# A windowed-attention and binary-FFN layer on one core: the order of the first and last attention blocks

## The chip, the cores and the metric

One core of a Trainium2 chip. The metric is the device time of one launch in microseconds (us); before the change the median of three runs was 380.07 us (380.04 to 381.41).

## The reference

A post-norm transformer layer over x of 4096 tokens x 256, all in float32:

```
q, k = l2norm(x Wq'), l2norm(x Wk')        16 heads of 16
v = x Wv'
p = softmax(q k' + bias)     bias = -slope[h]*|i-j|, -1e30 where j < i or j - i >= 128 (i query, j key)
x1 = layernorm(x + (p v) Wo')
bw = mean|w| over a row * sign(w)          for w1 (1024 x 256) and w2 (256 x 1024)
out = layernorm(x1 + gelu(x1 bw1' + b1) bw2' + b2)
```

The slopes fall from 1 to 1/256 over the heads; a token sees itself and the 127 tokens that follow it.

## The kernel before

The 4096 tokens are 32 blocks of 128 (NB = 32). Since a query sees keys only in its own block and the next one, the keys of block i serve the queries of block i and of the block before it. The bias is not added to the scores: the values are multiplied by a faded exponential of the slope ("fading", `fade_values`), so the exponential is taken of the bare scores, and GpSimd cuts the masked triangle out of it (`cut_tile`, an affine select). Queries and keys are split into a high and a low float16 part (`high_halves` on ScalarE, `low_halves` on GpSimd, `double` on VectorE copies the query part), and a transposing DMA turns them (`turn_parts`). Rows are normalised by a root from Ln and Exp on ScalarE (`root`) that three small VectorE operations refine (`round_of`).

Every engine runs its own list, written out by hand. Engines meet only at semaphores. `step(i, slot)` is one attention block on an engine. On TensorE (L427) it is: two of four score chunks, the output projection of block i-4, the strips of block i-3 turned, the query-key projection of block i+3, the rows of i-3 turned, the value projection of i+1, the other two score chunks, and the weighted sums of block i-2. On ScalarE (L645): strips of i-3 copied, exponentials 0 and 1, high halves of i+2, squares of i+3, rows of i-3 copied, exponentials 2 and 3, root. On VectorE (L927): round and normalised rows, addition of the projected output to the residual (`add_output`), normaliser and output rows (`outputs`), layer norm, `aside`, sums of squares, fading of block i+1, `amid`, doubled parts. On GpSimd (L1331): cuts of the block, with the low halves of block i+2 between chunk 1 and 2. SyncE issues the DMAs in order (L251).

Blocks 0 to 3 and 24 to 31 are written out, 4 to 23 are loops. Into the first blocks the kernel puts the signs of both weight matrices (ScalarE: `signs2` ahead of block 0, `signs1` behind blocks 2 and 3), into 24 to 31 the first rows for the FFN, the row sums of |w1|, a bound on the hidden values (`bound_rows`, turned by TensorE in `turn_bound`, its maximum taken in `take_bound`, spread over the partitions by a matmul in `spread_bound`), the scales from it (`scale_bound`, `hidden_scales`, `second_scale`, which ends with `prep`) and the first hidden products (`hidden(0, 0, 0)` in block 29, `hidden(0, 1, 0)` in block 31). Behind block 31 a tail finishes blocks 28 to 31 amid the other hidden products of group 0 (L573 to L593). Then come eight FFN groups of four blocks: 32 matmuls of hidden products and 64 of second products each. `keep_warm` issues matmuls whose result nobody reads, ahead of block 0.

TensorE waits for `resid_done` before it projects values (L398), since both projections write one PSUM bank; for `v_ready` before both; for `prep` before it projects block 28's output (L573).

## Time and profile before

| | |
|---|---|
| median of 3 runs | 380.07 us |
| the profiled execution | 379.94 us, its span 378.2 us |
| busy: TensorE | 357.4 us (94%) |
| VectorE | 325.3 us (86%) |
| ScalarE | 309.3 us (82%) |
| GpSimd | 275.0 us (73%) |
| chain that ended last | PE 71%, DVE 16%, ACT 5%, issue 5% |

Times inside the execution are counted from the start of the span. "Busy" is time in which an instruction of the engine ran. A row's idle time in brackets is the time in which the engine did nothing ahead of it, with the instruction that released it. PE is TensorE, DVE VectorE, ACT ScalarE, POOL GpSimd. One block of the loop takes 7.26 us. A float32 matmul appears as two entries.

### The profile page before, as it was taken

What the parts mean: (1) busy time and instruction counts of PE and PEld (TensorE: products, weight loads), DVE (VectorE), ACT (ScalarE), POOL (GpSimd) and SP (SyncE); (2) the same over time, 40 slices, a digit from 0 to 9 for tenths busy, and PEclk for the clock granted to TensorE, in tenths of its full rate; (3) what the DMA queues carried; (4) which work ended last, traced back from release to release, by engine and by line L of the source; (5) the groups of instructions that cost most, each with busy time, mean ns of one, the idle gap of its engine ahead of it and who ended that gap; (6) DMA issues with size and microseconds to landing.
All of it is one profiled execution on the core that took longest, in us unless ns stands there. A gap on an engine that the chain in (4) does not pass through costs nothing.

```text
span 378.2 us, 11990 instructions
## 1 busy us (share of the span) xinstructions
PE 357.4 (94%) x3921; PEld 243.2 (64%) x3921; DVE 325.3 (86%) x863; ACT 309.3 (82%) x536; POOL 275.0 (73%) x418
## 2 busy tenths in 40 slices
PE   8677999999999999999999999799999999999991
PEld 5534666766776776676677667575676667667671
DVE  3979698899889989888889999668689999999985
ACT  2688798898898898899899889587888888887773
POOL 1189699999999999999999998585455655654321
PEclk9999899999999999999999999999999999999998
DMA  7599845464455446346645653302112404404113
GB/s 230 117 255 237 139 87 96 114 123 99 111 108 114 99 105 129 85 109 129 149 112 102 126 106 65 57 3 57 36 22 56 105 9 112 108 16 100 57 56 111
DMA packets 98258, 38.31 MB, mean 101 GB/s; under 512 B 84656, under 2 KB 97328, under 8 KB 97968
## 3 DMA queue, kind: packets, MB, share of 16 engines
q1 hardware_dynamic: 98224, 37.89, 45.3%
q8 instruction: 17, 0.28, 0.3%
q14 instruction: 17, 0.14, 0.1%
HBM read 12.72 MB, written 4.19 MB: 45 GB/s over the span
## 4 chain that ended last, share of the span: by engine, by line
PE 71%; DVE 16%; ACT 5%; issue 5%; DMA 1%; DVEq 0%; SPq 0%
PE ps L514 13%; PE ps L552 13%; PE ps L381 10%; PE ps L391 10%; PE ps L361 6%; PE ps L423 6%; PE ps L400 5%; PE ps L408 3%; ACT prob L661 3%; DVE nt_b L829 2%; PE ps L415 2%; DVE rnorm L831 2%; DVE nt_a L827 1%; DMA qkT<-parts 1%; DVE ss L893 1%
## 5 line engine op out<-in xcount | busy, mean ns | idle before, releaser
L1307 POOL TENSOR_SCALAR_AFFINE_SELECT prob<-prob 128x512 f32<-128x512 f32 x252 | 154.8, 650 | 26.0 <-ACT prob L661 25.7
L661 ACT ACTIVATE prob<-ps 128x1024 f32<-128x1024 f32 (+1 forms) x128 | 122.1, 1008 | 15.9 <-PE ps L361 15.9
L391 PE MATMUL ps<-wqkv,xt 128*128 128x512 f32 x124 | 60.3, 609 | 1.9 <-DVE qkn L909 1.9
L726 ACT ACTIVATE ps<-ps,bias,alpha 128x512 f32<-128x512 f32 x64 | 47.9, 751 | 16.4 <-PE ps L514 13.2
L514 PE MATMUL ps<-yT,sgn 128*128 128x512 f16 x256 | 61.1, 379 | 0.0
L1374 POOL TENSOR_TENSOR resid<-z,resid 128x256 f32 (+1 forms) x31 | 22.5, 726 | 46.3 <-DVE z L1113 46.3
L381 PE MATMUL ps<-prob,vdiag 128*17 128x128 f32 x1024 | 51.3, 274 | 0.0
L381 PE MATMUL ps<-prob,vnext 128*17 128x128 f32 x992 | 49.9, 273 | 0.0
L361 PE MATMUL ps<-qkT 64*128 64x256 f16 (+1 forms) x512 | 39.2, 270 | 4.4 <-DMA qkT<-parts 2.9
L514 PEld LDWEIGHTS ps<-yT,sgn 128*128 128x128 f16 x256 | 25.1, 98 | 22.6
L423 PE MATMUL ps<-wo,oT 128*128 128x256 f32 x128 | 36.2, 405 | 0.9 <-ACT oT L642 0.6
L1327 POOL TENSOR_TENSOR parts<-qkn,parts 128x512 f16<-128x512 f32 x30 | 34.9, 1164 | 0.0
L361 PEld LDWEIGHTS ps<-qkT 64*128 64x128 f16 x512 | 19.4, 94 | 23.5 <-issue 13.8
L391 PEld LDWEIGHTS ps<-wqkv,xt 128*128 128x128 f32 x124 | 21.7, 195 | 19.3 <-issue 19.0
L400 PE MATMUL ps<-wqkv,xt 128*128 128x256 f32 x128 | 33.1, 381 | 0.7 <-DVE resid L849 0.7
L381 PEld LDWEIGHTS ps<-prob,vdiag 128*17 128x17 f32 x1024 | 26.2, 97 | 7.2 <-issue 7.2
L552 PE MATMUL ps<-sgn,w 128*128 128x256 f16 x256 | 30.6, 273 | 0.0
L552 PE MATMUL ps<-sgn,prob 128*128 128x256 f16 x256 | 30.2, 273 | 0.2 <-DVE prob L1103 0.2
L893 DVE TENSOR_REDUCE ss<-sq 128x32 f32<-128x512 f32 x32 | 21.9, 684 | 9.6 <-ACT sq L612 8.6
L612 ACT ACTIVATE sq<-ps 128x512 f32<-128x512 f32 x32 | 19.1, 596 | 12.5 <-PE ps L391 7.5
L552 PEld LDWEIGHTS ps<-sgn,w 128*128 128x128 f16 x256 | 25.1, 98 | 6.3
L552 PEld LDWEIGHTS ps<-sgn,prob 128*128 128x128 f16 x256 | 25.0, 98 | 5.9 <-DVE prob L1103 0.5
(114 smaller groups left out, 692.8 us busy)
## 6 DMA issues: line engine op xcount, KB each, us to landing
xt<-in_xT SPq DMA_DIRECT2D x32, 128.0 KB, 2.1
resid<-in_x SPq DMA_DIRECT2D x32, 128.0 KB, 2.2
out_dram<-resid SPq DMA_DIRECT2D x7, 512.0 KB, 2.9
w<-in_w2T SPq DMA_DIRECT2D x1, 1024.0 KB, 7.6
w<-in_w1T SPq DMA_DIRECT2D x1, 1024.0 KB, 6.5
w_nat<-in_w SPq DMA_DIRECT2D x2, 512.0 KB, 5.2
wqkv<-in_wqkvT SPq DMA_DIRECT2D x3, 256.0 KB, 4.4
qkT<-parts SPq DMA_TRANSPOSE x32, 4.3
```

What stands on the lines that cost most here:

```text
L361: mm = nc.tensor.matmul(ps[:, SC + 2 * (c % 2) + hp, 2 * P * t:2 * P * t + wide], qkT[row, here, H // 2 + 2 * c + t, :], queries, start=Tr ...
L381: mm = nc.tensor.matmul(ps[32 * m:32 * m + HD + 1, OT, P * c:P * c + P], v, p, start=(n == 0), stop=(n == 1 or not near))
L391: mm = nc.tensor.matmul(ps[:, QK[slot % 2], :], xt[:, slot, k, :], wqkv[:, k, 0:2 * D], start=(k == 0), stop=(k == DC - 1))
L400: mm = nc.tensor.matmul(ps[:, VO, 0:D], xt[:, slot, k, :], wqkv[:, k, 2 * D:3 * D], start=(k == 0), stop=(k == DC - 1))
L423: mm = nc.tensor.matmul(ps[:, VO, D:2 * D], oT[:, k, :], wo[:, k, :], start=(k == 0), stop=(k == DC - 1))
L514: mm = nc.tensor.matmul(ps[:, bank, :], sgn1[:, c, P * k:P * k + P], yT[:, par, a, c, :, :], start=(m == 0), stop=(m == 2 * DC - 1))
L552: mm = nc.tensor.matmul(ps[:, banks[b], 0:D], hid[par][:, a, k, P * b:P * b + P], sgn2[:, k, :], start=(m == 0), stop=(m == 2 * HC - 1))
L661: nc.scalar.activation(to, scored, ACT.Exp, scale=QK_SCALE ** -2).then_inc(exp_done, 1)
L726: nc.scalar.activation(bank, bank, ACT.Gelu, bias=bias1[:, k:k + 1], scale=alpha1[:, k:k + 1]).then_inc(gelu_done, 1)
L893: nc.vector.tensor_reduce(ss[:], sq[:].rearrange("p (h d) -> p h d", d=HD), AX.X, ALU.add).then_inc(ss_done, 1)
L1307: return nc.gpsimd.affine_select(out=at, in_=at, compare_op=ALU.is_ge, fill=0.0, base=-near, pattern=[[0, CH], [1 if near else -1, P]], ch ...
L1327: nc.gpsimd.tensor_tensor(parts[:, par, H:2 * H, 2:4, :], src[:, H:2 * H, :].unsqueeze(2).to_broadcast([P, H, 2, HD]), parts[:, par, H:2 * ...
```

## The change

TensorE: in blocks 0 and 2 the value projection goes behind the scores; block 1 gets six unread matmuls ahead of its end; in the last blocks the spreading of the bound and the second hidden product go one place on; the last three projected outputs each wait for the addition before. ScalarE: high halves ahead of the exponentials in block 0; the signs move to blocks 24 to 27 (w1 in four quarters) and 30 and 31 (w2 in two halves). VectorE: outputs ahead of the addition in every block; in the first and last blocks fading ahead of the sums, or ahead of the normalised row and the bound. GpSimd: low halves ahead of the cuts in blocks 0 and 2 to 4, one place ahead in block 1.

```diff
# TensorE
-            def project_out(q, values):
+            def project_out(q, values, added=0):
                 pe.wait_ge(ot_ready, q + 1)
                 pe.wait_ge(v_ready, values)
+                count(pe, resid_done, added)
...
-                if next1 and next3:
+                if next1 and next3 and not early:
                     project_v(i + 1, (slot + 1) % XS)
                 scores(i, 2, par, slot, both)
                 scores(i, 3, par, slot, both)
+                if early:
+                    project_v(i + 1, (slot + 1) % XS)
+                if behind:
+                    behind()
...
-            step(0, 0, out=False, strips=False, pv=False, both=False)
-            step(1, 1, out=False, strips=False, pv=False)
-            step(2, 2, out=False, strips=False)
+            step(0, 0, out=False, strips=False, pv=False, both=False, early=True)
+            step(1, 1, out=False, strips=False, pv=False, behind=lambda: keep_warm(WARM_BETWEEN, OT))
+            step(2, 2, out=False, strips=False, early=True)
...
-            step(NB - 2, 2, next3=False, amid=turn_bound, before_rows=spread_bound)
-            step(NB - 1, 3, next1=False, next3=False, amid=second_and_means)
+            step(NB - 2, 2, next3=False, amid=turn_bound)
+            step(NB - 1, 3, next1=False, next3=False, amid=spread_bound, before_rows=means)
             pe.wait_ge(prep, 1)
             project_out(NB - 4, NB)
             turn_strips(NB - 3)
+            second_hidden()
+            turn_rows(NB - 3)
             hidden(0, 2, 0)
-            turn_rows(NB - 3)
-            hidden(0, 3, 0)
             for c in range(NC):
                 weighted_sum(NB - 2, c, 2)
-            project_out(NB - 3, NB)
+            project_out(NB - 3, NB, NB - 3)
+            hidden(0, 3, 0)
...
# ScalarE
+                if high_first:
+                    high_halves(i + 2, par)
                 exps(0)
                 exps(1)
-                if next2:
+                if next2 and not high_first:
                     high_halves(i + 2, par)
...
-            signs2()
-            step(0, 0, strips=False, ln=False, both=False)
+            step(0, 0, strips=False, ln=False, both=False, high_first=True)
             step(1, 1, strips=False, ln=False)
-            step(2, 2, strips=False, ln=False, tail=lambda: signs1(0))
-            step(3, 3, ln=False, tail=lambda: signs1(1))
+            step(2, 2, strips=False, ln=False)
+            step(3, 3, ln=False)
...
-            step(NB - 8, 0, tail=lambda: high_y(0, 0, 0))
+            step(NB - 8, 0, amid=lambda: signs1(0), tail=lambda: high_y(0, 0, 0))
...
-            step(NB - 2, 2, next2=False, next3=False, tail=high_pair)
-            step(NB - 1, 3, next2=False, next3=False)
+            step(NB - 2, 2, next2=False, next3=False, amid=lambda: signs2(0), tail=high_pair)
+            step(NB - 1, 3, next2=False, next3=False, amid=lambda: signs2(1))
...
+            take_rows(NB - 1)
             high_hidden(0, 6, 0)
-            take_rows(NB - 1)
# VectorE
-                round_of(i - 1, prev3, prev_ln)
                 if prev3:
+                    round_of(i - 1, True, prev_ln)
                     normalise_rows(i + 2, par)
+                if strips:
+                    outputs(i - 3)
                 if out:
                     add_output(i - 4)
-                if strips:
-                    outputs(i - 3)
+                if aside:
+                    aside()
+                if next1 and not next3:
+                    fade_values(i + 1, (slot + 1) % XS)
+                if not prev3:
+                    round_of(i - 1, False, True)
                 if prev_ln:
                     y_row(i - 5, prev3)
...
-            step(1, 1, out=False, strips=False, prev_ln=False, ln=False)
+            round_of(0, True, False)
+            normalise_rows(3, 1)
+            fade_values(2, 2)
+            sums_of(4, False)
+            double(3, 1)
...
-            step(NB - 3, 1, next3=False, aside=bound_rows)
-            step(NB - 2, 2, prev3=False, next2=False, next3=False, amid=bounds)
-            step(NB - 1, 3, ..., aside=hidden_scales, amid=second_scale)
+            step(NB - 3, 1, next3=False, late=bound_rows)
+            step(NB - 2, 2, prev3=False, next2=False, next3=False, amid=take_bound)
+            step(NB - 1, 3, ..., aside=scales, amid=second_scale)
# GpSimd
-                for c in range(NC):
-                    cut_chunk(i, c, slot, both)
-                    if next2 and c == 1:
-                        low_halves(i + 2, slot % 2)
+                for c in range(NC):
+                    if next2 and c == low_at:
+                        low_halves(i + 2, slot % 2)
+                    cut_chunk(i, c, slot, both)
...
-            step(0, 0, both=False)
-            for n in range(1, XS):
-                step(n, n)
+            step(0, 0, both=False, low_at=0)
+            step(1, 1, low_at=1)
+            for n in range(2, 5):
+                step(n, n % XS, low_at=0)
```

## Rows read from the trace of the kernel before

**Rows 1.** busy time by stretch: A:B, length, engines' busy time (instructions), granted clock, DMA.
```profile
45.08:52.71 7.63, 7.48 (x103) 4.96 (x100) 6.85 (x16) 7.13 (x13) 6.40 (x11) 1.00 0.49 104
111.06:118.32 7.26, 7.26 (x103) 5.03 (x100) 6.41 (x17) 6.33 (x12) 6.72 (x11) 1.00 0.51 109
...
234.82:243.80 8.98, 6.51 (x103) 4.71 (x99) 5.71 (x18) 5.18 (x10) 5.49 (x10) 1.00 0.32 60
243.80:249.81 6.01, 6.01 (x101) 4.49 (x97) 4.15 (x14) 5.49 (x10) 4.03 (x7) 1.00 0.01 4
249.81:265.76 15.95, 15.15 (x159) 9.35 (x156) 13.02 (x29) 12.42 (x22) 10.47 (x16) 1.00 0.18 35
```

**Rows 2.** the same view in the first blocks.
```profile
38.00:39.00 1.00, 1.00 (x4) 0.57 (x3) 0.93 (x4) 1.00 (x2) 0.42 (x1) 0.50 1.37 182
```

**Rows 3.** timeline of PE, first blocks: start, length, engine, line, tiles, count, idle before.
```profile
14.12 3.29 PE L457 MATMUL ps<-mean_ones 128*128 128x128 f32 x28
...
28.59 0.91 PE L361 MATMUL ps<-qkT 64*128 64x256 f16 x8 [1.88 <-DMA qkT<-parts]
...
37.59 0.86 PE L408 MATMUL ps<-id,strips 128*128 128x128 f32 x4 [1.42 <-ACT strips L636]
38.23 3.42 PE L391 MATMUL ps<-wqkv,xt 128*128 128x512 f32 x4
...
47.40 1.88 PE L391 MATMUL ps<-wqkv,xt 128*128 128x512 f32 x4
```

**Rows 4.** timeline of ACT, first blocks.
```profile
32.47 0.42 ACT L626 ACTIVATE parts<-qkn 128x256 f16<-128x256 f32 x1 [1.21 <-DVE qkn L909]
...
36.01 1.04 ACT L694 ACTIVATE sgn<-w 128x1024 f16<-128x1024 f32 x1
36.95 0.58 ACT L636 ACTIVATE strips<-ps 128x512 f32<-128x512 f32 x1
```

**Rows 5.** timeline of DVE, first blocks.
```profile
28.64 0.41 DVE L884 TENSOR_TENSOR vdiag<-ps,fade 128x256 f32<-128x256 f32 x1
```

**Rows 6.** timeline of POOL, first blocks.
```profile
21.44 1.16 POOL L1327 TENSOR_TENSOR parts<-qkn,parts 128x512 f16<-128x512 f32 x1
```

**Rows 7.** timeline of DVE, PE and ACT in one loop block.
```profile
113.51 0.41 DVE L849 TENSOR_TENSOR resid<-resid,ps 128x256 f32 x1
113.84 0.25 DVE L839 RECIPROCAL rden<-ps 128x16 f32<-128x16 f32 x1
114.12 0.42 DVE L842 TENSOR_TENSOR otok<-ps,rden 128x256 f32<-128x256 f32 x1
...
114.94 1.03 PE L400 MATMUL ps<-wqkv,xt 128*128 128x256 f32 x4
...
116.34 1.94 ACT L661 ACTIVATE prob<-ps 128x1024 f32<-128x1024 f32 x2 [0.54 <-PE ps L361]
```

**Rows 8.** timelines of DVE and PE in blocks 25 to 27.
```profile
203.61 1.13 DVE L822 TENSOR_SCALAR half<-ss 128x32 f32<-128x32 f32 x1
...
208.44 0.41 DVE L849 TENSOR_TENSOR resid<-resid,ps 128x256 f32<-128x256 f32 x1
...
212.00 0.18 DVE L822 TENSOR_SCALAR half<-ss 128x32 f32<-128x32 f32 x1
...
209.53 0.44 PE L415 MATMUL ps<-id,otok 128*128 128x128 f32 x2 [0.29 <-DVE otok L842]
```

**Rows 9.** timelines of PE and DVE, blocks 29 to 31 and behind.
```profile
230.55 0.41 DVE L849 TENSOR_TENSOR resid<-resid,ps 128x256 f32<-128x256 f32 x1
...
231.11 1.10 PE L400 MATMUL ps<-wqkv,xt 128*128 128x256 f32 x4
...
238.11 1.10 PE L400 MATMUL ps<-wqkv,xt 128*128 128x256 f32 x4 [0.72 <-DVE resid L849]
240.66 0.38 PE L491 MATMUL ps<-bound_max,mean_ones 1*128 1x1 f32 x2 [1.45 <-DVE bound_max L994]
...
264.79 1.13 PE L423 MATMUL ps<-wo,oT 128*128 128x256 f32 x4 [0.59 <-ACT oT L642]
```

More of the change, by code:

```diff
@@ L46 @@
 WARM_AGAIN = 14
+WARM_BETWEEN = 6
 QSLOT = (0, 2, 1, 3)
@@ L425, in project_out, with step @@
                 mm.then_inc(wo_done, 1)
-            def step(i, slot, out=True, strips=True, pv=True, next1=True, next3=True, both=True, amid=None,
-                     before_rows=None):
+            def step(i, slot, out=True, strips=True, pv=True, next1=True, next3=True, both=True, early=False,
+                     amid=None, before_rows=None, behind=None):
                 par = slot % 2
@@ L452, in step, with keep_warm @@
                         weighted_sum(i - 2, c, (slot - 2) % XS)
-            def keep_warm(times):
+            def keep_warm(times, bank=SC):
                 for n in range(times):
-                    nc.tensor.matmul(ps[:, SC, 0:P], mean_ones[:], mean_ones[:], start=True, stop=True)
+                    nc.tensor.matmul(ps[:, bank, 0:P], mean_ones[:], mean_ones[:], start=True, stop=True)
             pe.wait_ge(layout, 1)
@@ L643, in take_rows, with step @@
                                      ACT.Copy).then_inc(ot_ready, 1)
-            def step(i, slot, strips=True, next2=True, next3=True, ln=True, both=True, amid=None, tail=None):
+            def step(i, slot, strips=True, next2=True, next3=True, ln=True, both=True, high_first=False, amid=None,
+                     tail=None):
                 par = slot % 2
@@ L686, in norm_of, with signs2, signs1 @@
                 root(half[:, cols], lnx[:, cols], rnorm[:, cols], newton, base, 1)
-            def signs2():
+            def signs2(half):
+                rows = slice(half * HC // 2, half * HC // 2 + HC // 2)
                 act.wait_ge(w2_in, 16)
-                nc.scalar.activation(sgn2[:], w2_t, ACT.Sign).then_inc(sgn_ready, 1)
-            def signs1(part):
+                nc.scalar.activation(sgn2[:, rows, :], w2_t[:, rows, :], ACT.Sign).then_inc(sgn_ready, 1)
+            def signs1(quarter):
+                cols = slice(quarter * HID // GB, quarter * HID // GB + HID // GB)
                 act.wait_ge(w1t_in, 16)
-                nc.scalar.activation(sgn1[:, part], w1_t[:, part], ACT.Sign).then_inc(sgn_ready, 1)
+                nc.scalar.activation(sgn1[:, :, cols], w1_t[:, :, cols], ACT.Sign).then_inc(sgn_ready, 1)
             nc.scalar.preload_act_table_set("natural_log_exp_and_others")
@@ L940, in step @@
                     layer_norm(i - 4)
-                if aside:
-                    aside()
+                if amid:
+                    amid()
                 if next3:
                     sums_of(i + 3, ln)
-                if next1:
-                    fade_values(i + 1, (slot + 1) % XS)
-                if amid:
-                    amid()
+                    if not double_first:
+                        fade_values(i + 1, (slot + 1) % XS)
                 if next2:
                     double(i + 2, par)
+                if double_first:
+                    fade_values(i + 1, (slot + 1) % XS)
+                if late:
+                    late()
             nc.vector.memset(mean_ones[:], 1.0 / HID).then_inc(layout, 1)
@@ L1028, in first_rows @@
                 nc.vector.tensor_scalar(bias2[:], bias2[:], Y_SCALE, None, ALU.mult).then_inc(bias_ready, 1)
[L1030 to L1032 removed]
+            round_of(0, True, False)
[3 more added lines that the diff above has]
+            double(3, 1)
+            step(2, 2, out=False, strips=False, prev_ln=False, ln=False, amid=third_quarter)
+            step(3, 3, out=False, prev_ln=False, ln=False, amid=last_quarter)
             dve.wait_ge(first_resid, 16 * 2)
             dve.wait_ge(second_resid, 16 * 2)
[L1035 removed]
+            step(4, 0, prev_ln=False, amid=first_rows)
             with dve.Fori(0, (NB - 12) // XS) as t:
@@ L1260, in finish_last @@
                                             ALU.subtract, ALU.mult).then_inc(last_row, 1)
+            outputs(NB - 3)
             add_output(NB - 4)
-            outputs(NB - 3)
             round_of(NB - 1, False, True)
@@ L1268, in _ @@
             hidden_low(0, 1, 0)
+            outputs(NB - 2)
             add_output(NB - 3)
-            outputs(NB - 2)
             row_stats(NB - 3, mv_late[:, 1, :])
@@ L1273, in _ @@
             hidden_low(0, 3, 0)
+            outputs(NB - 1)
             add_output(NB - 2)
-            outputs(NB - 1)
             hidden_low(0, 4, 0)
@@ L1384, in group_step @@
                         add_b2(g + 2, b)
-            step(NB - 8, 0, behind=lambda: low_y(0, 0, 0))
+            low_y(0, 0, 0)
             step(NB - 7, 1, behind=lambda: low_y(0, 1, 0))
```

41 lines of the change are left out of this document (18 added, 23 removed).

## The prediction

> **What bounds the kernel now.** I read busy time by stretch first, then the timelines where a stretch has a hole. In a block of the loop it is busy for all of its 7.26 us, VectorE for 6.41, ScalarE for 6.33 and GpSimd for 6.72 [rows 1]. So in the loop, and in the FFN groups behind, only TensorE's own work counts, and the change leaves that as it is but for six short matmuls. What can be won lies in the holes of the first blocks and of blocks 30, 31 and the tail. Block 4 starts at 45.08 and takes 7.63. Block 30 takes 8.98 of which TensorE works 6.51, block 31 takes 6.01 with no hole, and the tail up to the second group's first hidden product takes 15.95, of which 15.15 are busy [rows 1]. In the first blocks TensorE stands 1.88 ahead of block 2's scores and 1.42 ahead of turning block 0's strips [rows 3]. Right behind that the granted clock is 0.50, the 1.2 GHz level [rows 2], and the query-key projection of four matmuls takes 3.42 where the next one takes 1.88 [rows 3].
>
> **The start, step by step.** Block 2 waits at 28.59 for its transposing DMA, but what sets the pace behind it is the ring ScalarE, VectorE, ScalarE: squares, sums, root, rounds, normalised rows, high halves. ScalarE stands 1.21 for the normalised rows at 32.47 [rows 4].
>
> High halves ahead of the exponentials in block 0: they can start when the first transposing DMA has landed (block 0's scores start then, at 18.4) instead of at 19.7, so the low halves, whose key part takes 1.16 and began at 21.44 [rows 6], end about 1.5 earlier, and so does the issue of block 2's DMA. I take 1.0 of that as landed earlier (bounds 0 to 1.5). It is hidden: block 2's exponentials stand in line on ScalarE behind block 1's root, which I get at 29.2, and they began at 29.35. Price if that cover goes: none, only the gain is missed. The exponentials pushed back by the high halves cost nothing up to 20.7, since the next squares wait for the projection that ends there.
>
> Fading ahead of the sums in block 1: two instructions at 0.33 apiece until the next starts (0.41 long) [rows 5] leave the place between the sums' scaling and the doubled parts. With 0.3 won one block earlier I count 0.85 at ScalarE's high halves: 31.6 in place of 32.47. Bounds: 0.3, if the small operations run into GpSimd, to 1.2, ScalarE's whole wait.
>
> Signs out of blocks 2 and 3: a piece holds ScalarE from 36.01 to 36.95, 0.94 [rows 4], directly ahead of the strips that TensorE waits for. The large one before block 0 lay in idle time, worth nothing. Strips then begin at 36.95 - 0.85 - 0.94 + 0.15 (the root's input is now a little late) = 35.3, 1.65 earlier.
>
> Clock: TensorE's mostly idle stretch ahead of the strips shrinks from 2.2 to about 1.4, and the six warming matmuls fill 1.4 of the wait in block 1 (28 entries, 14 matmuls, took 3.29 [rows 3], so 0.235 each; block 2's scores can't start before 27.8 and the six end near 27.3; without that cover they would cost up to 1.4). I take it that the projection stays at full clock: 3.42 - 1.88 = 1.54 saved [rows 3]. But the rows of block 0 then wait for VectorE, whose rounds, block 5's normalised rows and the outputs are only some 0.5 earlier; about 0.6 comes back as a wait at 38.3, so 0.9 stays. Bounds 0 (dip stays) to 1.54.
>
> Block 4: the second sign piece leaves too, and 7.63 becomes the loop's 7.26 [rows 1]: 0.35. Sum of the start: 1.65 + 0.9 + 0.35 = **2.9** (bounds 1.2 to 3.9).
>
> Low halves ahead of the cuts on GpSimd in blocks 0 and 2 to 4: the cuts behind them come up to 1.8 later (a query and a key part). Weighted sums want a block's cuts one block on; I get them 2 us before that. No cost; without the cover up to 1.8 once.
>
> **The loop.** VectorE now does a block's outputs before it adds the projected output. TensorE has no hole at turned rows, so an earlier output wins nothing. The projection of values waits for the addition. The addition began at 113.51 and the outputs ended at 114.5 [rows 7]; with the addition (0.33 until the next starts, 0.41 long) behind them the wait is over near 114.55, and the projection starts at 114.94 anyway [rows 7]. It costs 0, with 0.4 to spare. In blocks 26 and 28 VectorE is late (the addition at 208.44, 3.02 after its block's start, where a loop block has 113.51 - 111.06 = 2.45) and TensorE stands 0.29 for the rows [rows 8]. There the new order frees the rows 0.33 earlier: 2 x 0.29 = 0.58 won (bounds 0 to 1.0).
>
> Four sign quarters in blocks 24 to 27, two halves in 30 and 31: a quarter is half a former piece, 0.47 plus some fixed part, 0.51 as I take it (at most 0.94). It goes between copied rows and the third exponentials, where ScalarE stands 0.54 [rows 7]. Covered, 0; uncovered 4 x 0.51 = 2.0.
>
> **The end.** Block 29: here the addition began at 230.55 and TensorE was at the projection of values by 231.11 [rows 9]. With the outputs in front (114.54 - 113.84 = 0.7, of which 0.65 until the next starts) the addition is through near 231.6: **0.5 lost** (0 to 0.65).
>
> Block 30: the wait of 1.45 for the bound's maximum, that of 0.72 for the addition [rows 9], and 0.3 at the projected output. The spreading matmul moves to block 31, so the 1.45 goes. Fading before the bound's five small operations (some 1.8 in all) frees the 0.3. The addition is late as before: outputs wait for turned strips at 237.3, so about 0.7 stays. From 235.3 I get to 242.0, 6.7 in place of 8.98: **2.3 won** (1.5 to 2.6).
>
> Block 31: this gives much back. The second scores wait for exponentials, which the first sign half (0.94) holds up: 0.4. Strips come 0.35 late behind them; the means wait for the addition behind the outputs, 0.75; and the scales, the round, the normalised row and the statistics now all stand before the second scale, so TensorE waits for it until 249.6, though its sums end at 249.0. From 242.0 to 249.6 is 7.6 in place of 6.01: **1.6 lost** (0.6 to 2.2). Named queue: behind that wait stand the projected output of block 28 and all that follows on TensorE.
>
> Tail: one hidden product moves in, four matmuls, 0.86. The wait of 0.59 for the last rows goes [rows 9], because they are copied before the high half of hidden chunk 6; nearly all other holes of the tail (0.8 busy time short of its length [rows 1], the 0.59 among them) are filled by that product. Chunk by chunk I get 265.05 from 249.6: 15.45 against 15.95, **0.5 won** (-0.3 to 0.8). The added waits for the additions of blocks 29 to 31 end before they are asked.
>
> Sum of the end: 0.58 - 0.5 + 2.3 - 1.6 + 0.5 = **1.3** (bounds -0.5 to 2.5). In all 4.2. The profiled execution took 379.94: 375.7. The median is 0.13 above it: **375.8**. Likeliest case's own range 374.3 to 377.3.
>
> **A rule against it.** Beside the key's low half (1.16 [rows 6]) a small scaling took 1.13, and 0.18 alone [rows 8]. So what an operation of VectorE costs depends on what GpSimd does at that moment, and the change moves just this 1.16 piece. The Trainium skill (SBUF — State Buffer, SBUF: two separate sides) says that the port pair the two engines share is "an exclusive lock, not a bandwidth split", held for the whole instruction; the trace's 1.13 agrees. By the rows, if in each of blocks 1 to 3 one more small operation of the ring takes 1.13 in place of 0.18, the start loses 3 x 0.95 = 2.85, nearly all it won, and 1.3 is left: 378.6. That is the third rival.
>
> **Rivals.**
> 1. The clock falls all the same in the first blocks (it fell to 0.50 after TensorE had stood 1.42, and had done little before; some 1.4 of that remains). For: the short hole is still there. Against: it did not fall after the 1.88 at block 2, nor after the 1.45 in block 30. Price 0.9 to 1.5: 377.0.
> 2. Slower: VectorE becomes late in the loop. The projection of values waits for the addition, which is now a place further back. The point from which it decides: normalised rows that end more than 2.85 after the block's start (now 2.45; in block 26 it was 3.02). If the new start leaves GpSimd's cuts in a phase in which all 20 loop blocks look like block 26, which took 7.76 in place of 7.26, that is 20 x 0.5 = 10 us: 385.7. Against: the loop has kept one phase for 20 blocks, and TensorE's pace draws it back.
> 3. The collisions above: 378.6, no change.
> 4. More is won: the end gives back only 0.6 in block 31 and the whole clock saving stays: 373.5.
>
> **How the numbers follow.** Forecast 0.50, first rival 0.20, slower 0.06, no change 0.13, more 0.11. A difference of 0.5%, 1.9 us, is what can be told: faster is below 378.2. The forecast, its first and fourth rivals lie there nearly whole, with a little of the third: 0.82. Within: most of the third and the edge of the others, 0.12. Slower 0.06. The range takes in the fourth and the third: 373.4 to 378.7; outside are the slower case and a few tails.
>
> **What would show it.** Right: block 4's scores near 42.5, strips of block 0 at 35.3, projection of block 6 at 1.9 and not 3.4; loop at 7.26; no hole at turned rows in 26 and 28; block 30 near 6.7, block 31 near 7.6, with a wait ahead of block 28's projected output; span near 374.0. Wrong: a loop period above 7.26, block 4 after 44, exponentials in 24 to 27 that follow a sign directly with TensorE waiting, or 30 and 31 together above 15.0.

## The result: 0.5% faster, less than half of the forecast gain

| us | before | changed |
|---|---|---|
| median (runs) | 380.06 (10) | 378.18 (10) |
| lowest to highest | 378.62 to 381.41 | 377.56 to 379.29 |
| profiled execution | 379.94 | 377.56 |
| its span | 378.2 | 375.9 |
| TensorE busy | 357.4 (94%) | 357.8 (95%) |

The ratio is 0.9949, interval 0.9931 to 0.9967. The forecast was 375.8, a gain of 4.2; the median gained 1.9. The direction was right, the size was not. Beside the experiments the runs of the kernel before lie in three groups, near 378.1, 380 and 381.4, and only the middle one has a profile; the changed kernel's lie within 377.56 to 379.29, so part of the median's gain is how often the upper groups come, and what sets them apart is open.

Windows of the changed kernel, by stretch from one block's first scores to the next's: blocks 4 to 6, 24, 26, 29 to 31, and the tail (from the projected output of block 28 to the second group's first hidden product). They answer to [rows 1].

```profile
41.77:49.25 7.48, 7.48 (x102) 4.98 (x100) 6.60 (x16) 6.40 (x12) 6.68 (x11) 1.00 0.49 104
49.25:57.33 8.08, 7.69 (x102) 4.99 (x100) 7.64 (x19) 6.32 (x12) 8.08 (x14) 1.00 0.49 103
57.33:64.64 7.31, 7.31 (x103) 5.07 (x100) 6.92 (x18) 6.42 (x12) 6.81 (x11) 1.00 0.64 112
188.02:195.28 7.26, 7.26 (x102) 5.04 (x99) 6.50 (x16) 6.91 (x13) 6.69 (x11) 1.00 0.77 111
202.54:210.20 7.66, 7.66 (x102) 4.98 (x99) 7.34 (x18) 7.12 (x14) 7.32 (x12) 1.00 0.50 107
225.12:232.36 7.24, 6.69 (x103) 4.81 (x100) 5.32 (x14) 6.02 (x11) 6.70 (x11) 1.00 0.40 75
232.36:239.44 7.08, 5.96 (x99) 4.55 (x96) 5.13 (x20) 5.42 (x10) 4.01 (x8) 1.00 0.41 76
239.44:246.97 7.53, 6.13 (x99) 4.19 (x95) 4.13 (x16) 6.46 (x12) 4.35 (x8) 1.00 0.01 3
246.97:263.38 16.41, 15.92 (x158) 9.74 (x159) 12.41 (x27) 12.66 (x22) 11.01 (x17) 1.00 0.17 34
```

Block 4 starts 3.31 earlier on the clock of the trace. 0.64 of that is in place before block 0's scores (17.79, 18.43 before): the very first projection took 2.45, before 3.11, with a wait of TensorE's weight load for the DMA of wqkv in it (0.53, before 1.10). From the second projection to block 0's scores both kernels take 10.8. I don't count it to the change, since another kernel below with the same instructions up to there (the one without warming) has 3.17 for the first projection and 18.51 for the scores. So the start won 2.67. From block 4's scores to block 24's there are 146.25 (145.82 before), so 0.43 is given back, all of it in blocks 4 to 6: 22.87 for the three, 22.43 before. From the projected output in block 24 to the second group's first hidden product the changed kernel takes 74.82, before 74.32. The end, which was to win 1.3, **lost 0.5** (a plus is longer): block 29 +0.63, block 30 -1.90, block 31 +1.52, tail +0.46, and -0.10 in each of blocks 26 and 28. What follows takes the same, 112.5 in both. Together -2.67 + 0.43 + 0.50 - 0.64 = -2.38; the spans, rounded to 378.2 and 375.9, differ by 2.3.

First blocks, timeline of TensorE in the changed kernel (start, busy, line, operation, idle before and what ended it). It answers to [rows 3].

```profile
28.15 0.61 PE L363 MATMUL ps<-qkT 64*128 64x256 f16 x8 [1.14 <-DMA qkT<-parts]
28.91 1.98 PE L393 MATMUL ps<-wqkv,xt 128*128 128x512 f32 x4
...
35.09 0.66 PE L410 MATMUL ps<-id,strips 128*128 128x128 f32 x4 [0.18 <-ACT strips L640]
35.58 1.88 PE L393 MATMUL ps<-wqkv,xt 128*128 128x512 f32 x4
38.12 0.44 PE L417 MATMUL ps<-id,otok 128*128 128x128 f32 x2 [0.65 <-DVE otok L850]
38.39 1.03 PE L402 MATMUL ps<-wqkv,xt 128*128 128x256 f32 x4
...
41.77 0.50 PE L363 MATMUL ps<-qkT 64*128 64x256 f16 x6
...
53.46 0.44 PE L417 MATMUL ps<-id,otok 128*128 128x128 f32 x2 [0.39 <-DVE otok L850]
```

The wait ahead of block 0's strips was 1.42 and is 0.18. The projection behind them took 3.42 and takes 1.88. Of this, 0.65 has come back as a wait for the rows of block 0.

ScalarE, the same kernel: the wait ahead of block 0's high halves, where the signs of w2 had stood, the strips, a sign quarter in block 24 and the two sign halves in blocks 30 and 31.

```profile
17.74 0.42 ACT L630 ACTIVATE parts<-qkn 128x256 f16<-128x256 f32 x1 [2.00 <-DMA qkT<-parts]
...
34.44 0.60 ACT L640 ACTIVATE strips<-ps 128x512 f32<-128x512 f32 x1
...
192.65 0.63 ACT L703 ACTIVATE sgn<-w 128x512 f16<-128x512 f32 x1
193.30 1.02 ACT L666 ACTIVATE prob<-ps 128x1024 f32<-128x1024 f32 x1
...
237.33 1.05 ACT L698 ACTIVATE sgn<-w 128x1024 f16<-128x1024 f32 x1
238.28 1.93 ACT L666 ACTIVATE prob<-ps 128x1024 f32<-128x1024 f32 x2
...
244.78 1.05 ACT L698 ACTIVATE sgn<-w 128x1024 f16<-128x1024 f32 x1
...
247.88 0.58 ACT L640 ACTIVATE strips<-ps 128x512 f32<-128x512 f32 x1
```

TensorE, blocks 29 to the tail, where it waits. This answers to [rows 9].

```profile
228.64 1.10 PE L402 MATMUL ps<-wqkv,xt 128*128 128x256 f32 x4 [0.55 <-DVE resid L857]
...
235.69 1.10 PE L402 MATMUL ps<-wqkv,xt 128*128 128x256 f32 x4 [1.12 <-DVE resid L857]
...
240.27 0.39 PE L363 MATMUL ps<-qkT 64*128 64x256 f16 x4 [0.43 <-ACT prob L666]
...
243.57 0.67 PE L540 MATMUL ps<-w_sum,mean_ones 128*128 128x256 f32 x2 [0.92 <-DVE resid L857]
...
248.52 0.66 PE L410 MATMUL ps<-id,strips 128*128 128x128 f32 x4 [0.42 <-ACT strips L640]
```

Three waits end with the addition (L857), which stands behind the outputs now, and two with work of ScalarE that stands behind a sign half. These five, 3.44 in all, are what is left to explain at the end.

### The profile page after: what moved, and what is told of

Its sections match the earlier page's. It is cut to its first block, busy times and chain, and to the rows that moved or that the text cites. A ratio compares the mean times of both kernels' runs of the same rounds, so it can differ in the third digit from the quotient of the medians.

```text
span 375.9 us, 12012 instructions
## 1 busy us (share of the span) xinstructions
PE 357.8 (95%) x3933; PEld 243.8 (65%) x3933; DVE 325.4 (87%) x863; ACT 309.5 (82%) x539; POOL 274.8 (73%) x418
## 4 chain that ended last, share of the span: by engine, by line
PE 79%; DVE 9%; ACT 6%; issue 3%; DMA 1%; POOL 0%; DVEq 0%; POOLq 0%; SPq 0%; ACTq 0%
PE ps L521 14%; PE ps L560 13%; PE ps L383 12%; PE ps L393 11%; PE ps L426 8%; PE ps L363 7%; PE ps L402 7%; PE ps L410 3%; ACT prob L666 3%; PE ps L417 2%; DMA qkT<-parts 1%; DVE nt_b L837 1%; PE ps L464 1%; DVE rnorm L839 1%; DVE ss L901 1%
## 5 line engine op out<-in xcount | busy, mean ns | idle before, releaser
L393 PE MATMUL ps<-wqkv,xt 128*128 128x512 f32 x124 | 58.7, 596 | 2.1 <-DVE qkn L917 1.9
L402 PE MATMUL ps<-wqkv,xt 128*128 128x256 f32 x128 | 33.6, 385 | 1.7 <-DVE resid L857 1.7
L383 PEld LDWEIGHTS ps<-prob,vnext 128*17 128x17 f32 x992 | 28.3, 98 | 0.0
L1376 POOL TENSOR_TENSOR yparts<-resid,yparts 128x256 f16<-128x256 f32 (+1 forms) x32 | 21.2, 684 | 9.3 <-ACT yparts L728 9.2
```

Source lines behind the costliest of these rows:

```text
L383: mm = nc.tensor.matmul(ps[32 * m:32 * m + HD + 1, OT, P * c:P * c + P], v, p, start=(n == 0), stop=(n == 1 or not near))
L393: mm = nc.tensor.matmul(ps[:, QK[slot % 2], :], xt[:, slot, k, :], wqkv[:, k, 0:2 * D], start=(k == 0), stop=(k == DC - 1))
L402: mm = nc.tensor.matmul(ps[:, VO, 0:D], xt[:, slot, k, :], wqkv[:, k, 2 * D:3 * D], start=(k == 0), stop=(k == DC - 1))
```

## The experiments

Diffs are against the changed kernel unless another is named, and "..." marks what is left out. The kernel before ran beside each; its single runs lay between 377.70 and 381.50, its medians between 379.63 and 380.13. "The end" is the stretch from the projected output that follows block 24's first scores to the second group's first hidden product, from one profile of each kernel.

**1. The start alone.** The kernel before with the changed first blocks (all engines) and the signs late; ends of TensorE, VectorE and GpSimd as before, outputs behind the addition. The diff is against the kernel before; ScalarE's last steps and TensorE's counts of the signs go with it, and VectorE and GpSimd have their first blocks as changed.

```diff
-            signs2()
-            step(0, 0, strips=False, ln=False, both=False)
+            step(0, 0, strips=False, ln=False, both=False, high_first=True)
...
-            step(2, 2, strips=False, ln=False, tail=lambda: signs1(0))
-            step(3, 3, ln=False, tail=lambda: signs1(1))
+            step(2, 2, strips=False, ln=False)
+            step(3, 3, ln=False)
...
-            step(NB - 1, 3, next2=False, next3=False)
+            step(NB - 1, 3, next2=False, next3=False, amid=lambda: signs2(1))
```

> The kernel before with the first blocks of the change and the signs moved to blocks 24 to 27, 30 and 31; the order of VectorE in the loop, the bound, the last blocks and the tail as before. Theory A (what the two traces suggest: the start wins 2.2 from block 0's scores to block 24's, and a sign half of 0.94 behind the copied rows of blocks 30 and 31 lies on the path): 0.4 to 1.3 us faster than before, blocks 30 and 31 together 0.9 to 1.9 longer than the 15.0 of before. Rival B (the forecast's own terms: signs covered everywhere but 0.4 in block 31): 2.2 to 2.9 us faster, blocks 30 and 31 together at most 15.4.

Measured 379.86 (378.80 to 380.54), ratio 0.9993 (0.9968 to 1.0018). That is 0.27 under the kernel before and not clear of noise, less than both theories had. In its profile the end takes 76.00, 1.68 more than before, and all of it stands behind the w2 signs: 0.80 in blocks 30 and 31 (15.79, before 14.99), 0.89 in the tail (16.84). From block 0's scores to block 24's the profile is 1.32 shorter than before, with the clock down in it at block 2 (below). So the start does not carry the gain by itself: the signs it pushes out are paid at the end.

**2. The end alone.** The changed kernel with first blocks and all signs as before, on all four engines (outputs stay ahead of the addition). Of the diff, ScalarE's part:

```diff
-            step(0, 0, strips=False, ln=False, both=False, high_first=True)
+            signs2(0)
+            signs2(1)
+            step(0, 0, strips=False, ln=False, both=False)
...
-            step(3, 3, ln=False)
+            step(3, 3, ln=False, tail=lambda: (signs1(2), signs1(3)))
```

> The changed kernel with the first blocks as before and all signs in them again; loop order, bound, last blocks and tail as changed. Theory A (the changed end loses 0.5 with the signs in it and 0.85 of that is theirs): within 0.6 us of before, blocks 24 to the tail 0 to 0.6 shorter than before. Rival B (the forecast: the end wins 1.3 with the signs in it): 1.7 to 2.2 us faster.

Measured 377.40 (377.07 to 379.30), ratio 0.9947 (0.9918 to 0.9976): as fast as the whole change, or faster, and 2.7 under the kernel before beside it, more than either theory had. Its end takes 73.39, 0.93 less than before. The rest of the 2.85 between the two profiles' spans is not the end's: 0.85 lies ahead of block 0's scores (17.58, before 18.43), and 1.08 between these and block 24's, where the first blocks are those of before but for the order of outputs and addition. The clock fell at another place there: against block 0's scores the strips are turned 0.64 later (19.80, before 19.16), and the projection behind them takes 1.88 in place of 3.42, together 0.90 less. Experiment 11, with the order of outputs and addition alone, has 0.12 of the rest.

**3. Low halves of block 4 back behind two cuts.** For the 8.08 of block 5.

```diff
-            for n in range(2, 5):
-                step(n, n % XS, low_at=0)
+            for n in range(2, 4):
+                step(n, n, low_at=0)
+            step(4, 0)
```

> The changed kernel, with GpSimd's low halves of block 4 between chunk 1 and 2 as in the loop. Theory A (block 5 takes 8.08 because twelve cuts run back to back beside VectorE's small operations, and they do because block 4's cuts stand behind the low halves): block 5 at 7.26 to 7.5, block 4's scores where they were, 0.5 to 0.9 us faster than the changed kernel. Rival B (VectorE is late because outputs stand ahead of the addition): block 5 stays above 7.9, no change.

Measured 378.40 (377.48 to 379.36), ratio 0.9953 (0.9927 to 0.9979). Block 5 still took 8.22, so it isn't this low half; that theory fell. (Rival B's reason falls too: experiments 1 and 12 have the addition first there, and 8.02 and 8.08 in block 5.) The profile showed something else: here the clock fell after all, at another place.

Timeline of TensorE and windows of this kernel (columns as in [rows 1]; the last but two is the granted clock: 0.99, 0.58 and 1.00).

```profile
29.84 3.68 PE L393 MATMUL ps<-wqkv,xt 128*128 128x512 f32 x4
```

```profile
28.00:30.00 2.00, 0.77 (x9) 0.47 (x10) 1.87 (x4) 0.86 (x4) 2.00 (x4) 0.99 1.15 343
30.00:34.00 4.00, 4.00 (x13) 1.24 (x13) 1.76 (x3) 2.75 (x5) 2.79 (x5) 0.58 1.08 226
34.00:36.00 2.00, 2.00 (x42) 1.62 (x44) 1.78 (x4) 2.00 (x4) 2.00 (x5) 1.00 0.85 284
```

**4. The addition first again in blocks 29 to 31.**

```diff
+                late_block = isinstance(i, int) and i >= NB - 3
-                if strips:
+                if strips and not late_block:
                     outputs(i - 3)
                 if out:
                     add_output(i - 4)
+                if strips and late_block:
+                    outputs(i - 3)
```

> The changed kernel, with VectorE's addition ahead of the outputs again in blocks 29 to 31 alone. Theory A (TensorE stands 0.55, 1.12 and 0.92 there for the addition, which has its input long before): these waits go, blocks 29 to 31 together 21.85 - 2.0 to 2.5, and 1.5 to 2.5 us faster than the changed kernel. Rival B (the rows come 0.33 later and TensorE waits for them or for exponentials in place of it): 0 to 0.7 us faster.

Measured 376.20 (375.38 to 376.82), ratio 0.9892 (0.9849 to 0.9934): 2.0 under the changed kernel. TensorE in this kernel, the same places:

```profile
228.72 1.10 PE L402 MATMUL ps<-wqkv,xt 128*128 128x256 f32 x4
...
234.81 1.10 PE L402 MATMUL ps<-wqkv,xt 128*128 128x256 f32 x4
...
239.38 0.39 PE L363 MATMUL ps<-qkT 64*128 64x256 f16 x4 [0.43 <-ACT prob L666]
...
241.69 0.70 PE L540 MATMUL ps<-w_sum,mean_ones 128*128 128x256 f32 x2
...
246.09 1.13 PE L426 MATMUL ps<-wo,oT 128*128 128x256 f32 x4 [0.92 <-DVE alpha L1095]
```

The three waits for the addition (2.59) are gone, and so is the 0.42 ahead of the strips in the tail. A new wait of 0.92 stands ahead of the projected output of block 28, for the second scale; it is at the place where the forecast had put one. Blocks 29 to 31 take 20.27 in place of 21.85, 1.58 less where theory A had 2.0 to 2.5, and the tail another 0.64 less. The end takes 72.60, 2.22 less. Windows of the tail and of a stretch ahead of block 0 in this kernel:

```profile
246.09:261.87 15.78, 15.71 (x159) 9.82 (x160) 12.20 (x27) 11.83 (x20) 10.42 (x16) 1.00 0.18 35
12.00:14.00 2.00, 2.00 (x5) 1.04 (x4) 1.65 (x6) 0.87 (x3) 0.00 (x0) 0.50 0.05 10
```

The tail is that short with both sign halves still in blocks 30 and 31. The second row shows the clock at half in a place where the changed kernel has it at full.

**5. The signs of w2 at the start again**, both halves ahead of block 0 on ScalarE.

```diff
+            signs2(0)
+            signs2(1)
             step(0, 0, strips=False, ln=False, both=False, high_first=True)
...
-            step(NB - 2, 2, ..., amid=lambda: signs2(0), tail=high_pair)
-            step(NB - 1, 3, next2=False, next3=False, amid=lambda: signs2(1))
+            step(NB - 2, 2, ..., tail=high_pair)
+            step(NB - 1, 3, next2=False, next3=False)
```

> The changed kernel with both halves of w2's signs ahead of block 0 again (w1's quarters stay in 24 to 27). Theory A (in the profile ScalarE stands 2.0 us ahead of block 0's high halves, so the halves are free there, and lie on the path in 30 and 31): blocks 30, 31 and the tail 0.9 to 1.5 shorter, 0.9 to 1.6 us faster than the changed kernel. Rival B (at the end they are covered but for 0.4, the forecast's term): 0 to 0.5 us faster.

Measured 376.83 (376.00 to 377.28), ratio 0.9929 (0.9908 to 0.9950): 1.35 under the changed kernel. ScalarE at the start and the windows of block 31 and of the tail in this kernel:

```profile
16.09 1.99 ACT L698 ACTIVATE sgn<-w 128x1024 f16<-128x1024 f32 x2
17.98 0.40 ACT L630 ACTIVATE parts<-qkn 128x256 f16<-128x256 f32 x1
```

```profile
239.78:246.63 6.85, 5.88 (x99) 4.27 (x95) 4.15 (x16) 5.75 (x12) 4.08 (x8) 1.00 0.02 4
246.63:262.41 15.78, 15.71 (x159) 9.83 (x159) 12.18 (x27) 11.80 (x20) 10.40 (x16) 1.00 0.18 35
```

At the start the halves fill the stretch in which ScalarE stood 2.00 for the transposing DMA. At the end block 31 takes 0.68 less and the tail 0.63 less, together 1.31, which is the gain of the median.

**6. No warming** in block 1.

```diff
-            step(1, 1, out=False, strips=False, pv=False, behind=lambda: keep_warm(WARM_BETWEEN, OT))
+            step(1, 1, out=False, strips=False, pv=False)
```

> The changed kernel without the six unread matmuls in block 1. Theory A (what sets a run's time in the first blocks is whether TensorE's clock falls to half there, and these matmuls make that rarer): the median rises by 0.5 to 2 us and the runs spread over 3 us as those of the kernel before do. Rival B (they do nothing for the clock): same median as the changed kernel within 0.3 and the same spread, 377.5 to 379.3.

Measured 378.50 (377.88 to 379.38), ratio 0.9979 (0.9955 to 1.0004), 0.3 above the changed kernel with ranges that overlap nearly whole. In its profile TensorE stands still for 3.00 ahead of block 2's scores, where the kernel before had 1.88, and the clock did not fall behind it (the projection that follows takes 1.98, the full-clock length):

```profile
29.20 0.61 PE L363 MATMUL ps<-qkT 64*128 64x256 f16 x8 [3.00 <-DMA qkT<-parts]
```

Nothing shows that the six matmuls are worth anything, and a gain of 0.3 isn't excluded.

**7. All signs at the start.** As 5, and w1's quarters in pairs behind blocks 2 and 3, none late.

```diff
-            step(2, 2, strips=False, ln=False)
-            step(3, 3, ln=False)
+            step(2, 2, strips=False, ln=False, tail=lambda: (signs1(0), signs1(1)))
+            step(3, 3, ln=False, tail=lambda: (signs1(2), signs1(3)))
...
-            step(NB - 8, 0, amid=lambda: signs1(0), tail=lambda: high_y(0, 0, 0))
+            step(NB - 8, 0, tail=lambda: high_y(0, 0, 0))
```

> The changed kernel with all signs in the first blocks, as before (w2's ahead of block 0, w1's two quarters each behind blocks 2 and 3). With e5 it prices w1's pieces. Theory A (a piece of 0.94 stands right ahead of the strips in block 2 and 3): block 4's scores 0.9 later than in the changed kernel in a run with full clock, 0.7 to 1.2 us slower than e5. Rival B (block 3's rows wait for VectorE anyway and take most of it up): within 0.4 us of e5.

Measured 377.52 (376.82 to 379.11), ratio 0.9960 (0.9934 to 0.9985), 0.7 above experiment 5: that is what w1's pieces cost between the first blocks. It is not paid where theory A had it. Block 4's scores come 23.99 after block 0's, as in the changed kernel (23.98); blocks 4 to 6 are long instead, 23.14. Experiment 2 has the same signs and the old order of the first blocks, and its median is 377.40. So the reordering of the first blocks alone shows no effect on the median. In the profiles there is one: from block 0's scores to block 24's this kernel takes 0.87 less than experiment 2, but its block 0 starts 0.91 later (18.49 against 17.58), behind a first projection of 3.14 against 2.21. Whether the medians carry such a difference too is not shown.

**8. Experiments 4 and 5 together, and the second scale earlier** (called inside `scales`, ahead of the round of the statistics). The third edit against 4 and 5 together:

```diff
+                second_scale()
...
-            step(NB - 1, 3, ..., aside=scales, amid=second_scale)
+            step(NB - 1, 3, ..., aside=scales)
```

> The changed kernel with the addition first in blocks 29 to 31, w2's signs ahead of block 0, and the second scale right behind the other scales in block 31. Theory A (the holes are independent: 1.9 from the addition, 1.2 from the signs, 0.5 to 0.9 from the wait ahead of block 28's projected output): 374.6, 3.2 to 4 us faster than the changed kernel. Rival B (one hole opens as the other closes): 375.8, about where e4 is.

Measured 375.40 (374.40 to 375.78), ratio 0.9899 (0.9863 to 0.9935). TensorE and ScalarE in this kernel:

```profile
244.32 1.13 PE L426 MATMUL ps<-wo,oT 128*128 128x256 f32 x4
246.24 0.66 PE L410 MATMUL ps<-id,strips 128*128 128x128 f32 x4 [0.78 <-ACT strips L640]
```

```profile
245.26 0.20 ACT L621 ACTIVATE lnx<-half 128x1 f32<-128x1 f32 x1 [1.02 <-DVE half L832]
245.49 0.20 ACT L623 ACTIVATE rnorm<-lnx 128x1 f32<-128x1 f32 x1
245.60 0.58 ACT L640 ACTIVATE strips<-ps 128x512 f32<-128x512 f32 x1
```

The wait for the second scale is gone and 0.78 stands ahead of turning the strips of block 29: ScalarE, ahead of copying them, waits 1.02 for the halved variance that VectorE now makes later. The gain on the changed kernel is 2.8, between theory A (3.2 to 4) and rival B (2.4).

**9. The same without that third edit:** the two diffs of 4 and 5 and nothing else.

> The changed kernel with the addition first in blocks 29 to 31 and w2's signs ahead of block 0; the second scale where the change has it (e8 without its third edit). Theory A (e8's third edit only moved the hole: TensorE's wait of 0.92 ahead of block 28's projected output became one of 0.78 ahead of turning block 29's strips): 375.2 to 375.6, as e8. Rival B (the third edit cost the tail the 1.0 by which e8's is longer than e4's): 374.4 to 374.8.

Measured 375.36 (375.15 to 376.32), ratio 0.9884 (0.9852 to 0.9916). Same time, so the third edit is worth nothing: block 31 and the tail take 7.26 and 15.78 here, 6.09 and 16.78 with it. The two gains add up to 2.82 of 3.33 (1.98 and 1.35).

**10. Experiment 9 with the rows of the bound prepared in block 29** and not in block 4.

```diff
-            step(4, 0, prev_ln=False, amid=first_rows)
+            step(4, 0, prev_ln=False)
...
-            step(NB - 3, 1, next3=False, late=bound_rows)
+            step(NB - 3, 1, next3=False, aside=first_rows, late=bound_rows)
```

> As e9, and VectorE's third row sum of |w1| with the scaling of b2 (1.2 us) moved from block 4 to block 29, ahead of the fading. Theory A (blocks 4 and 5, 14.75 to 15.56 in the profiles where two loop blocks take 14.52, are long because VectorE has this 1.2 more to do there and then runs its small operations beside GpSimd's cuts): blocks 4 and 5 together at most 14.7, 0.3 to 1.0 us faster than e9. Rival B (it is the start's order itself): blocks 4 and 5 stay above 15.0 in the profile, no gain.

Measured 375.20 (374.80 to 375.69), ratio 0.9869 (0.9838 to 0.9900). That is the lowest median of the study, but 0.2 under experiment 9 is less than the spread. Blocks 4 to 6 took 7.47, 7.42 and 7.66: block 5 is short and block 6 long, 22.55 together where experiment 9 has 22.82. Blocks 4 and 5 together are 14.9, between what the two theories had.

**11. The kernel before with outputs ahead of the addition**, nothing else.

```diff
-                if out:
-                    add_output(i - 4)
                 if strips:
                     outputs(i - 3)
+                if out:
+                    add_output(i - 4)
```

> The kernel before with one edit: VectorE's outputs ahead of the addition in every block. It asks where the slow runs of the kernel before come from (its runs lie near 378.1, 380 and 381.4; e2, with nearly the same first blocks, lies at 377.3 with a few at 379). Theory A (rows of block 0 and 1 come earlier, and TensorE's clock falls less often in the first blocks): median 378.0 to 378.8, no runs near 381.4. Rival B (the order does nothing there): the three groups stay, median 379.5 to 380.5.

Measured 379.58 (378.59 to 380.55), ratio 0.9984 (0.9961 to 1.0007). The median is as rival B had it, but its twelve runs lie in neither outer group: 6 of the 17 runs of the kernel before beside it lay from 380.90 to 381.48, and 5 from 378.02 to 378.37. Blocks 26 and 28 took 7.65 and 7.66 in place of 7.76 and 7.77, and the end 74.97 in place of 74.32.

**12. The changed kernel with the addition first in every block.**

```diff
-                if strips:
-                    outputs(i - 3)
                 if out:
                     add_output(i - 4)
+                if strips:
+                    outputs(i - 3)
```

> The changed kernel with the addition ahead of the outputs in every block (e4 has it in blocks 29 to 31 only). Theory A (in the loop the order is worth nothing, in blocks 26 and 28 it was worth 0.1 each): 376.2 to 376.6, as e4. Rival B (the forecast's term of 0.29 per block holds, or the first blocks need the outputs first): 376.8 or more.

Measured 376.10 (375.51 to 376.56), ratio 0.9895 (0.9864 to 0.9927), as experiment 4. In the loop the order of the two is worth nothing that shows; only the last blocks tell.

## Why the forecast was right in direction and wrong in size

**The start, forecast 2.9.** Up to block 4 the steps held. High halves, fading and signs brought the strips to 34.44; with the 0.64 that came ahead of block 0 taken off, the forecast's 35.3 reads 34.7. The projection took 1.88 as forecast, and the wait for rows came back with 0.65 against 0.6. That makes 2.67 where the working had 2.55 up to there. The **last term failed: block 4 at the loop's 7.26, 0.35 won**. It took 7.48 and block 5 8.08, so 0.4 was lost in blocks 4 to 6. VectorE in block 5 of the changed kernel, and GpSimd beside it:

```profile
50.17 0.62 DVE L835 TENSOR_TENSOR nt_a<-half,rnorm 128x33 f32<-128x33 f32 x1
50.83 0.55 DVE L837 TENSOR_TENSOR nt_b<-nt_a,rnorm 128x33 f32<-128x33 f32 x1
51.41 0.56 DVE L839 SCALAR_TENSOR_TENSOR rnorm<-nt_b,rnorm 128x33 f32<-128x33 f32 x1
52.09 0.69 DVE L917 TENSOR_TENSOR qkn<-ps,rnorm 128x512 f32<-128x512 f32 x1
52.70 0.25 DVE L847 RECIPROCAL rden<-ps 128x16 f32<-128x16 f32 x1
```

```profile
47.65 7.26 POOL L1326 TENSOR_SCALAR_AFFINE_SELECT prob<-prob 128x512 f32<-128x512 f32 x12
```

The outputs wait behind three small operations that each take as long as one of the twelve cuts that GpSimd does without a gap (7.26 / 12 = 0.6). VectorE also comes to them late, 0.92 after the block's start (50.17 - 49.25), where a loop block has 0.37 (111.43 - 111.06 before) and 0.20, 0.53 and 0.55 for the three. TensorE then stands 0.39 for the rows. This is the third rival's mechanism at a small size, two blocks later than it was placed. It is not the low halves (experiment 3) and not the outputs' place (experiments 1 and 12 have the old one, and 8.02 and 8.08 in block 5). VectorE's 1.2 of preparing rows in block 4 has a part in block 5, which is 7.42 without it, but block 6 is then 7.66 (experiment 10). That the phase of VectorE against GpSimd's cuts decides it is argued, not shown. With the same code in blocks 4 to 6 the three took 22.03 (experiment 5) to 22.87; where they are short, in experiments 4 to 6 (22.39, 22.03, 22.05), TensorE had stood 0.41 to 0.80 for a transposing DMA right ahead of block 4's scores, so that part of the difference only stands elsewhere. From block 0's scores to block 7's all kernels with the new first blocks and full clock there took 46.5 to 47.2, the changed kernel 46.85, the kernel before 49.08.

**The clock.** In this profile it stayed up, as forecast, but that is no property of the change. In the profiles of experiments 1 to 3 it fell near block 2 (the projection there took 3.52, 3.13 and 3.68; experiment 3 has the changed kernel's instructions up to that place), and in that of experiment 11 where it fell before. In those of experiments 4 and 5 it fell ahead of block 0 (granted clock 0.50 and 0.52 from 12 to 14), where the changed kernel has the same TensorE instructions; block 0's scores came 11.36 after the second projection there and 10.8 in all the others, so it cost 0.57. In those of 6 to 10 and 12 it did not fall. One profile each can't tell how often. Each run's mean granted clock is on record: in the changed kernel's ten it was 0.994 in those of 377.56 (the profiled one) and 377.69, and 0.989 in those of 378.81 and 379.29. That fits a clock that fell in some of them; no trace shows where. The forecast took one profile of each as the median; here the changed kernel's profiled run was its fastest, 0.62 under its median, and the one of before lay 0.12 under its own. The first rival's price is thus paid in some kernels' runs and not in others. The fourth rival came in neither half: the clock's saving stayed in this profile, and the end gave back more, not less.

**The loop and the sign quarters, forecast 0.** Right: 7.26 from block 7 to block 25 and in block 27, a quarter (0.63, the next starts after 0.65; I had 0.51) in ScalarE's gap. The slower rival did not occur.

**Blocks 26 and 28, forecast 0.58, measured 0.20.** The rows came without a wait, but the projection of values behind them waited: L417 at 206.34 and L402 at 206.76, where the two follow each other after 0.27 at 38.12. The wait moved one step on. Experiment 11 has the same 0.1 a block.

**Block 29, forecast -0.5, measured -0.63; block 30, +2.3 and +1.90; block 31, -1.6 and -1.52** (here and in the next paragraph a plus is a gain). These terms held within 0.4. Block 30 won less because the wait for the addition was 1.12 and not 0.7. Block 31's hit is in part luck. The working had TensorE's sums end 7.0 after the block's start and a wait of 0.6 for the second scale behind them; the sums ended 7.5 after it, and there was no wait ahead of block 28's projected output, which was one of the signs of being right. The wait of 0.92 appears there once the waits for the addition are gone (experiment 4). Experiment 4 shows that the new order costs 2.0 from block 29 on (2.22 of the end in the profile), for nothing won elsewhere (experiment 12). The working charged it with 0.5 and 0.75, 1.25 in all; the 0.7 in block 30 it took as there in either order, and with the old order that wait is gone too.

**The tail, forecast +0.5, measured -0.46.** This is **the step that failed most, 0.96**. The working took it that the added product would fill the tail's holes and leave 15.45; 16.41 was measured. Two things were wrong.
- The sum contradicted its own rows. 15.15 busy [rows 1] and 0.86 for the added product are 16.01, and no filled hole can make 15.45 of that. Measured were 15.92 busy and 0.49 idle. Without the idle time it is 15.78, of it 15.71 busy (some operations took a little less). It is so with the w2 signs away (experiment 5) and also with them in place, once the addition is first (experiments 4 and 12).
- The second sign half had no term. It stands in block 31 ahead of exponentials, and the strips behind these come late in the tail (the wait of 0.42). Taking both halves away won 0.68 in block 31 and 0.63 in the tail; the working had 0.75 for the one and nothing for the other. The tail's part is not the sign half's alone: in experiment 4 TensorE stands 0.92 for the second scale, the strips are copied by then, and the tail is as short. It is lost where TensorE comes to the strips before ScalarE.

The sentence on w2's signs, "lay in idle time, worth nothing", was true of their old place. It should have been followed to the end: work that costs nothing where it is can only lose by moving. It lost 1.35 (experiment 5).

**The sum.** In the profiles the end missed by 1.8 (tail 0.96, blocks 26 and 28 0.38, block 30 0.40, block 29 0.13, less 0.08 in block 31) and the start by 0.66 (0.78 in blocks 4 to 6, less 0.12 ahead), while 0.64 came from ahead of block 0: together 1.8. The changed kernel's median, 0.62 above its profiled run and not 0.13, is the other 0.5. The causes of the end's part are shown by experiments 4 and 5: taking both back gives 375.36 (experiment 9), under the forecast's 375.8. The cause of the start's part is not shown.

**The page against it.** The Trainium skill (SBUF — State Buffer, SBUF: two separate sides) calls the shared port an exclusive lock held for an instruction. The trace agrees: the first two of the three small operations took 0.17 and 0.19 in the kernel before at 23.96 and 24.17, between two runs of cuts, with GpSimd idle, and take 0.62 and 0.55 beside cuts of 0.6, as above. I weighed the rule only against the 1.16 low half in the first blocks; it bore on the continuous cuts behind them.

**Open:** how often the clock falls and where in each kernel; what makes the three groups of the kernel before; what sets blocks 4 to 6 between 22.0 and 23.1; whether the warming matmuls are worth 0.3; and the 0.2 of experiment 10.

## What to carry to other kernels

Before adding up a stretch in which work moves, take its busy time plus what moves in as a floor. It is good to a few tenths (16.01 here, where 15.78 was the least measured), and a forecast well below it (15.45) is an error of arithmetic that can be found without a chip. Follow each moved piece at both ends: ask first whether its old place cost anything, and give every instruction behind its new place a term, also in the next stretch. An order that suits the loop may be dear in the last blocks, where the engine that used to hide it has less work of its own: test the two apart.

## What the chip showed that I had not expected

- The same instructions up to block 0's scores ended at 17.79 in one kernel and at 18.51 in another; over all kernels they lay between 17.58 and 18.51. The difference is made in two places: the first projection, which waits for the DMA of wqkv, took 2.21 to 3.17, and in experiments 4 and 5 the low clock added 0.57. Single profiles can thus differ by 0.9 before the edited part begins.
- The granted clock fell near 38 in the kernel before (0.50), and from 30 to 34 in experiment 3 (0.58 over that window), where TensorE had been busy 0.77 of the 2 us ahead. The wait right ahead does not tell. The clock fell behind waits of 1.42 to 1.97 in seven profiles and stayed up behind one of 3.00 in experiment 6; and behind the wait of 1.92 that every kernel has ahead of the third projection (10.81 in the changed kernel) it fell in two profiles of fourteen. The low stretch lengthens the matmuls it falls on by 1.5 to 1.8, but the kernel only by what no wait behind it takes up: 0.57 ahead of block 0, where the changed kernel waits 1.04 for a DMA and experiments 4 and 5 do not.
- A run of small dependent operations on VectorE can be slowed as a whole beside continuous cuts: 0.62, 0.55 and 0.56 one after the other in block 5, where a loop block of the kernel before has 0.20, 0.53 and 0.55.
